# An unrolled two-layer gated FFN on one core: a longer warm-up, six pieces of work moved along the step list, half 1's normalisation shared with ScalarE, and the last half stored tile by tile

## What is computed

```python
x = x + xattn(layernorm(x), token_ids, ctx, ctx, ctx)   # 4 experts, chosen by token id
x = x + ffn(layernorm(x), Wg, W1, W2, W3)               # 8 experts, top 2 by score

def xattn(h, ids, Wg, Wu, Wd):          # Wg = Wu = Wd = ctx, F = D = 256
    e_of = minimum(ids // 3125, 3)
    y_e = (silu(h @ Wg[e].T) * (h @ Wu[e].T)) @ Wd[e].T
    return y_e where e_of == e

def ffn(h, Wg, W1, W2, W3):             # hidden size 176 for each expert
    w = softmax over the two largest of (h @ Wg.T), 0 elsewhere
    return sum over e of w[e] * ((silu(h @ W1[e].T) * (h @ W2[e].T)) @ W3[e].T)
```

## Time and profile before

| what | value |
|---|---|
| median of 3 runs | 166.15 us (165.05 to 166.26) |
| the profiled execution | 166.07 us |
| its span, first to last instruction | 164.3 us |
| PE busy | 153.7 us (94%) |
| DVE busy | 113.8 us (69%) |
| ACT busy | 66.9 us (41%) |
| POOL busy | 58.8 us (36%) |

### The profile page before, as it was taken

One profiled execution on the slowest core, in us unless ns is written; L12 is line 12 of the kernel. 1 busy time (PEld: TensorE's weight loads), 2 busy tenths in 40 slices (PEclk: granted clock), 3 DMA queues, 4 the chain that ended last, 5 costly groups with the idle time before them and its releaser, 6 DMA issues.

```text
span 164.3 us, 2431 instructions
## 1 busy us (share of the span) xinstructions
PE 153.7 (94%) x892; PEld 130.9 (80%) x892; DVE 113.8 (69%) x223; ACT 66.9 (41%) x119; POOL 58.8 (36%) x49
## 2 busy tenths in 40 slices
PE   7399999789998999899999999999999999999991
PEld 2188799768987788688888778898888888888890
DVE  0858999885895867799999796926444744444452
ACT  3366862753518544444438522315222222222210
POOL 0579967369765772459437300000000000000000
PEclk9969999999999999999999999999999999999999
DMA  3976263031130003330000000000000300000003
GB/s 113 345 256 169 70 209 108 0 96 33 70 96 0 2 0 100 96 94 1 0 0 4 0 0 2 0 4 0 0 0 0 129 3 0 0 0 4 2 0 128
DMA packets 4332, 8.76 MB, mean 53 GB/s; under 512 B 736, under 2 KB 864, under 8 KB 4320
## 3 DMA queue, kind: packets, MB, share of 16 engines
q1 hardware_dynamic: 4176, 8.60, 16.6%
q10 hardware_dynamic: 144, 0.00, 0.0%
HBM read 7.55 MB, written 1.05 MB: 52 GB/s over the span
## 4 chain that ended last, share of the span: by engine, by line
PE 63%; DVE 24%; ACT 3%; issue 3%; DMA 3%; POOL 1%; SPq 1%; ACTq 0%; DVEq 0%; POOLq 0%
PE z L675 35%; PE y L700 24%; DVE act_lo L543 5%; DVE act L578 4%; DVE norm L476 3%; DMA raw<-weights_dram 3%; DVE w_lo L549 2%; DVE hT_lo L483 2%; DVE stats L459 2%; PE y L618 1%; DVE x_sb L489 1%; DVE gate_rows L532 1%; ACT act_hi L382 1%; PE y L631 1%; POOL rstd L294 1%
## 5 line engine op out<-in xcount | busy, mean ns | idle before, releaser
L675 PE MATMUL z<-hT_hi,w_hi 128*128 128x512 f32 x120 | 47.7, 397 | 1.0 <-ACT hT_hi L356 0.8
L675 PE MATMUL z<-hT_hi,w_lo 128*128 128x512 f32 x120 | 47.2, 393 | 0.0
L700 PE MATMUL y<-w_hi,act_lo 128*128 128x256 f32 x152 | 43.5, 286 | 1.2 <-DVE act_lo L543 1.2
L543 DVE TENSOR_TENSOR act_lo<-act,act_hi 128x512 fp32r<-128x512 f32 x38 | 32.9, 867 | 14.9 <-ACT act_hi L382 14.7
L700 PE MATMUL y<-w_hi,act_hi 128*128 128x256 f32 x152 | 43.0, 283 | 0.0
L700 PE MATMUL y<-w_lo,act_hi 128*128 128x256 f32 x152 | 43.0, 283 | 0.0
L410 ACT ACTIVATE silu<-z 128x512 f32<-128x512 f32 x38 | 22.6, 596 | 41.7 <-PE z L675 41.6
L675 PE MATMUL z<-hT_lo,w_hi 128*128 128x512 f32 x120 | 37.5, 393 | 0.4 <-DVE hT_lo L483 0.3
L284 POOL TENSOR_TENSOR w_lo<-raw,w_hi 128x768 fp32r<-128x768 f32 (+1 forms) x15 | 28.3, 1891 | 15.0 <-ACT w_hi L347 14.9
L382 ACT CAST act_hi<-act 128x512 fp32r<-128x512 f32 x38 | 23.4, 617 | 23.0 <-DVE act L578 22.7
L700 PEld LDWEIGHTS y<-w_hi,act_lo 128*128 128x128 f32 x152 | 29.0, 191 | 3.3 <-DVE act_lo L543 1.9
(11 more groups left out here) (51 smaller groups left out, 82.0 us busy)
## 6 DMA issues: line engine op xcount, KB each, us to landing
raw<-weights_dram SPq DMA_DIRECT2D x11, 384.0 KB, 3.1
raw<-weights_dram SPq DMA_DIRECT2D x8, 256.0 KB, 4.7
x_sb<-x_dram SPq DMA_DIRECT2D x4, 256.0 KB, 4.7
out_dram<-x_sb SPq DMA_DIRECT2D x4, 256.0 KB, 2.5
consts_sb<-consts_dram SPq DMA_DIRECT2D x1, 68.0 KB, 3.8
ids_sb<-token_ids_dram ACTq DMA_DIRECT2D x1, 4.0 KB, 3.9
router_raw<-router_dram SPq DMA_DIRECT2D x1, 8.0 KB, 2.7
```

Of the source, the lines that this page charges most:

```text
L543: nc.vector.tensor_tensor(act_lo[:, i, :], act[:, i, :], act_hi[:, i, :].bitcast(F32), ALU.subtract)\
L675: return nc.tensor.matmul(bank[:], w[b][:, c, cols], tokens[:, h, k, :], **flags)
L700: last = nc.tensor.matmul(o, a[:, q % BUFFERS, rows], w[b][:, c, wd], start=(first and j == 0), stop=(c == CHUNKS[b] - 1 and j == 2), skip ...
```

## The change

Seven edits. The first six are in the amount of warm-up and in the order and placing of work, the last in how the end is written:

1. WARM goes from 12 to 24 matmuls.
2. GpSimd waits for VectorE's `w_lo` of piece (0, 0) before its own first ones.
3. The normalisation of half 1 in layer 1 (step 4) is shared as in layer 2: two tiles stay on VectorE, two go to ScalarE. With it come one `minus_mean` on VectorE and one `shift` on GpSimd.
4. ROUTER_STEP goes from 6 to 10.
5. The pieces (1, 4) to (1, 10) are split one step later: steps 16 to 22 where it was 15 to 21.
6. `tokens_lo` of layer 2, half 1 goes from step 21 to step 22 on VectorE.
7. The last half is added in four tiles of 256 columns, with one semaphore count for each tile of the last down step, and each tile is stored with a transfer of its own (128 KB), tiles 0 and 2 from SP, tiles 1 and 3 from ScalarE's queue.

```diff
-WARM = 12
+WARM = 24
...
-    "tokens_lo": (6, 4, 5),
+    "tokens_lo": (6, 4, 6),
...
-SPLIT_AT |= {FIRST[1, 0] + c - 5: ((1, c),) for c in range(4, CHUNKS[1])}
+SPLIT_AT |= {FIRST[1, 0] + c - 4: ((1, c),) for c in range(4, CHUNKS[1])}
...
-ROUTER_STEP = 6
+ROUTER_STEP = 10
...
+            for i in (0, 2):
+                t = HALF_TILES + i
+                sp.wait_ge(tile_ready, i + 1)
+                sp.dma_start(out_v[:, t, :], out_sb[:, t, :]).then_inc(stored, 16)
...
             inverse_deviation(0, 0)
+
+            pool.wait_ge(w_lo_vector, 1)
             for c in range(FIRST_PIECES):
...
                 for bb, hh in due("inverse_deviation", q):
                     inverse_deviation(bb, hh)
-                    if bb == 1:
-                        scaled_mean(hh)
+                    scaled_mean(bb, hh)
...
                 for bb, hh in due("normalise", q):
-                    if bb == 1:
-                        normalise_rest(hh)
+                    normalise_rest(bb, hh, (x_sb, x2_sb)[bb])
             round_act(NSTEPS - 1)
+            for i in (1, 3):
+                t = HALF_TILES + i
+                act_e.wait_ge(tile_ready, i + 1)
+                act_e.dma_start(out_v[:, t, :], out_sb[:, t, :]).then_inc(stored, 16)
...
-                        if b == 1:
+                        if ln_no(b, h):
                             nc.vector.tensor_scalar(minus_mean[:, cols], mv[:, cols, 0], -1.0, None, ALU.mult)
...
-                for i, t in list(enumerate(tiles_of(h)))[:DVE_TILES if b else HALF_TILES]:
+                for i, t in list(enumerate(tiles_of(h)))[:DVE_TILES if ln_no(b, h) else HALF_TILES]:
...
-            for i in range(2):
-                if i == 0:
-                    dve.wait_ge(last_first_bank, 1)
-                else:
-                    dve.wait_ge(down_done, NSTEPS)
-                add_bank(1, i, x2_sb, out_sb, out_ready)
+            for i in range(HALF_TILES):
+                t = HALF_TILES + i
+
+                dve.wait_ge(last_tiles, 2 * (i // 2) + 2)
+                nc.vector.tensor_tensor(out_sb[:, t, :], y[1][i // 2][:, (i % 2) * D:(i % 2 + 1) * D], x2_sb[:, t, :],
+                                        ALU.add).then_inc(tile_ready, 1)
...
-                    if q == NSTEPS - 1 and i == 1:
-                        last.then_inc(last_first_bank, 1)
-                last.then_inc(down_done, 1)
+                    if q == NSTEPS - 1:
+                        last.then_inc(last_tiles, 1)
+                if q < NSTEPS - 1:
+                    last.then_inc(down_done, 1)
```

More of the change, by code:

```diff
@@ L199, in ffn_moe @@
         act_hi_done, act_lo_done = sem("act_hi_done"), sem("act_lo_done")
-        down_done, last_first_bank = sem("down_done"), sem("last_first_bank")
+        down_done, last_tiles, tile_ready = sem("down_done"), sem("last_tiles"), sem("tile_ready")
         warm_in, x2_done, out_ready, stored = sem("warm_in"), sem("x2_done"), sem("out_ready"), sem("stored")
@@ L270, in _ @@
                 load_piece(1, c)
-            for pair in range(TILES // 2):
+            for pair in range(TILES // 4):
                 sp.wait_ge(out_ready, pair + 1)
@@ L275, in _ @@
                 sp.dma_start(out_v[:, tiles, :], out_sb[:, tiles, :]).then_inc(stored, 16)
-            sp.wait_ge(stored, 16 * (TILES // 2))
+            for i in (0, 2):
+                t = HALF_TILES + i
+                sp.wait_ge(tile_ready, i + 1)
+                sp.dma_start(out_v[:, t, :], out_sb[:, t, :]).then_inc(stored, 16)
+            sp.wait_ge(stored, 16 * (TILES // 4 + HALF_TILES))
         @block.gpsimd
@@ L295, in inverse_deviation, with scaled_mean @@
                             .then_inc(rstd_done, 1)
-            def scaled_mean(h):
-                pool.wait_ge(rstd_done, ln_part_no(ln_no(1, h), h * HALF_TILES))
+            def scaled_mean(b, h):
+                pool.wait_ge(rstd_done, ln_part_no(ln_no(b, h), h * HALF_TILES))
                 cols = slice(h * HALF_TILES + DVE_TILES, (h + 1) * HALF_TILES)
@@ L356, in tokens_hi, with normalise_rest @@
                     nc.scalar.copy(hT_hi[:, h, k, :], y[h][k][:]).then_inc(hT_hi_done, 1)
-            def normalise_rest(h):
-                act_e.wait_ge(shift_done, h + 1)
-                act_e.wait_ge(rstd_done, ln_part_no(ln_no(1, h), h * HALF_TILES))
-                act_e.wait_ge(norm_T, KD * ln_no(1, h))
+            def normalise_rest(b, h, src):
+                act_e.wait_ge(shift_done, ln_no(b, h))
+                act_e.wait_ge(rstd_done, ln_part_no(ln_no(b, h), h * HALF_TILES))
+                act_e.wait_ge(norm_T, KD * ln_no(b, h))
                 for i in range(DVE_TILES, HALF_TILES):
                     t = h * HALF_TILES + i
-                    nc.scalar.activation(norm[:, i, :], x2_sb[:, t, :], ACT.Identity, bias=shift[:, t:t + 1],
+                    nc.scalar.activation(norm[:, i, :], src[:, t, :], ACT.Identity, bias=shift[:, t:t + 1],
                                          scale=rstd[:, t:t + 1]).then_inc(norm_act, 1)
@@ L623, in transpose_tokens @@
                     for i in range(HALF_TILES):
-                        if b == 0:
-                            pe.wait_ge(norm_done, HALF_TILES * h + i + 1)
+                        n = ln_no(b, h)
+                        if n == 0:
+                            pe.wait_ge(norm_done, i + 1)
                         elif i < DVE_TILES:
-                            pe.wait_ge(norm_done, 2 * HALF_TILES + DVE_TILES * h + i + 1)
+                            pe.wait_ge(norm_done, HALF_TILES + DVE_TILES * (n - 1) + i + 1)
                         else:
-                            pe.wait_ge(norm_act, (HALF_TILES - DVE_TILES) * h + i - DVE_TILES + 1)
+                            pe.wait_ge(norm_act, (HALF_TILES - DVE_TILES) * (n - 1) + i - DVE_TILES + 1)
                         last = nc.tensor.transpose(y[h][k][:, i * P:(i + 1) * P], norm[:, i, k * P:(k + 1) * P], ident)
```

## The result

The changed kernel takes 164.48 us (median of 8 runs, 164.04 to 165.00). The kernel before took 166.14 in the 8 runs beside it (165.05 to 166.26). The ratio is 0.991, with a 95% interval from 0.9885 to 0.9934: 0.9% less, as forecast (164.6). The profiled execution of the changed kernel took 164.04 and is the lowest of its 8, its span is 162.2. So the profiles differ by 2.07 in their spans, and the medians by 1.66. One step of the working was wrong by more than 1 us all the same; two smaller errors, and the difference between the profiled run and the median, made up for it.

A forecast was written before the change was run, and what follows sets the result against it. TensorE was taken to bound the kernel (63% of the chain of waits, VectorE 24%), its stalls lying in the first hundred us. Six terms sum to -1.47: span 164.3 to 162.8, time 164.6 us, range 163.0 to 166.2.

The forecast's parts named there:

- Start: Edits 1 and 2, up to D1: faster clock for the transposes, less the new shift on GpSimd; -0.5, between -0.8 and +0.1.
- rival B: At the start, the clock stays low between 8 and 11 or extra matmuls are slow: 165.2 us; chance 0.15.
- Half 1 of layer 1: Edits 3 and 4, around U8: hT_lo follows hT_hi at once and U8 starts 0.12 earlier; -1.14, between -1.0 and -2.2.
- Step 10: Edit 4, path to D11: the router's subtraction waits for GpSimd ahead of half 0's statistics; +0.76, between -0.4 and +3.0.
- rival A: VectorE's act_lo wins one or both lock races, at 27.3 and 43.4: 163.5 or 162.4 us; chance 0.30.
- Gates: Edit 5, gates and U18: VectorE's copies no longer meet w_lo, U18 starts at about 68.2; -0.97, down to -0.5.
- Step 22: Edit 6, router's matmuls for half 1: three VectorE operations come ahead of hT_lo; +0.68, between +0.3 and +1.3.
- End: Edit 7, last adds and stores: the first store leaves 0.3 earlier, so the last data lands earlier; -0.3, other end +1.1.
- Rival C: GpSimd's operations fall twice into the path to D11: 3.0 instead of 0.76, time 166.9 us; chance 0.10.

The follow-up runs named there:

- the version with step 12: Changed kernel with the router's split in step 12 instead of 10 and tokens_lo of layer 2, half 1 back in step 21: 163.27 us, ratio 0.9862 to before.
- the version with slot 5: Changed kernel with only tokens_lo of layer 2, half 1 put back from step 22 to step 21: 163.56 us, ratio 0.9868 to before.
- step 13: Changed kernel with the router's split in step 13 instead of 10 and tokens_lo of layer 2, half 1 back in step 21: 163.75 us, ratio 0.989 to before.

## Why the prediction was right, and where it was not

**Start (forecast -0.5, measured -0.45): right, under a condition I had put in rival B.** The clock stayed up, `hT_hi` started at 9.31 (I had 8.95), and the wait at D1 grew only from 0.54 to 0.59, since U0 gained 0.69 and not 1.0. The 24 matmuls ended at 8.40, not 8.15, because in this run ten of them ran at the lower clock and in the profile of before nine; the added twelve were all fast. The transposes then started at 8.24 (I had 8.13), and eight of them stand ahead of `hT_hi`, 1.07 where I had left 0.8. The price of `shift` was right (0.26, I had 0.25). That edit 2 costs nothing was wrong: it costs GpSimd 0.2. In this profile VectorE's first `w_lo` came 0.24 earlier than in that of before with 24 matmuls (8.39 and 8.63), which hid this in the sum. What else I got wrong is how often there is something to gain. Most runs of the kernel before that I had seen were of the dropped kind (two of three times near 166.2, the profile too), yet of the 61 later runs in the table 32 were not, and against those edit 1 gains nothing. The Trainium skill, TensorE: Matmul & The Clock Gate, Part 1, had warned that the moment at which the clock changes varies from run to run of one kernel. The runs bear it out: the warm loads change their pace at 4.5 in the profile of before, at 4.99 in that of the changed kernel and at 7.07 in that of the version with step 12.

**Half 1 of layer 1 (forecast -1.14, measured -1.08): right.** `hT_lo` follows `hT_hi`, U8 takes 1.56, and `act_lo` of step 4 lost the port to `gated`, so edit 3 moved nearly nothing. The run with edit 3 undone and the one with the router back confirm which edit did what. Within the term two errors cancel: U8 to D5 shrank by 0.84, not 1.02, and D1 to U8 by 0.24, not 0.12 (0.12 by edit 4, as before with that edit alone shows, and 0.12 by edit 3).

**Step 10 (forecast +0.76, measured -0.40): this is the step that failed.** I wrote that "the cast delays `w_lo` by 0.11, not 0.16, so I keep the order of before". I compared the small delay with the small margin of the earlier trace rows and took VectorE's `act_lo` as fixed. But its time hung on two adds ahead of it, and these waited for TensorE, which edit 4 itself brings 0.5 forward against `act` there. With that wait gone, `act_lo` leads by 0.45, and the stretch comes out at the -0.4 that I had named as the other outcome. The reversed order and the wait that went give 0.92 (18.63 to the 17.71 of the version without the subtraction in that stretch, in which TensorE has next to no wait left); I had put it at 1.2 in the text. The subtraction did meet GpSimd, but its `w_lo` and not the `gated` that I had named, at 0.52 on the path instead of 0.76. So one half of rival A came true, and for a reason: it was no toss-up of 0.16, and of its two races the one at 27.3 went as I had said.

**Gates (forecast -0.97, measured -0.70): right in kind, too large by 0.27.** The copies took 0.63 and TensorE came to them without a wait. But "`gated` is made beside D14" was not so: ScalarE's copy starts when the transposes end (65.02), `gated` ends at 66.39, and D14 is through 0.3 earlier. I had counted D14 at 1.43, as if U18 could follow at once.

**Step 22 (forecast +0.68, measured +0.69): right.** The starts of three VectorE operations, one behind the other, and nothing hidden behind it; the version with slot 5 gives 0.7 back.

**End (forecast -0.3, measured -0.1): too large.** The first store does leave 0.27 earlier, but the transfers are then no faster than the engines, and 1 KB packets keep these busy longer. From the first data packet to the end of the last it is 1.66 (159.31 to 160.97), before 1.56 (161.54 to 163.10):

```profile
160.00:160.50 0.50, 0.00 (x0) 0.00 (x0) 0.00 (x0) 0.00 (x0) 0.00 (x0) 1.00 1.04 336
```

The DMA engines are busy all the time (1.04 by the window) at 336 GB/s, against 0.96 at 361 in the earlier trace rows. The other end of my range, +1.1 (each half-sized packet as long as a whole one), did not come either.

**The sum.** The terms measured add up to -2.05, mine to -1.47. Step 10 alone is -1.16 of the difference, the gates and the end give back 0.27 and 0.2. The medians moved by 1.66, less than the profiles, because the changed kernel's profiled run was its best, 0.44 under the median, and that of before only 0.07 under. So the forecast of 164.6 is near 164.48 largely by luck: an error of 1.16 at step 10, 0.46 the other way at the gates and the end, and 0.4 that the profiles and the medians differ by. The shape of the rivals served better than the sum: rival A, with one race won, had the mechanism.

Rival B (clock) fell as a story of this profile, but half of it holds for the comparison: before often starts with the clock up. Rival C fell: GpSimd was in the way once, not twice.

## What to carry to other kernels

Where two engines race for a shared port, don't look at the margin between the two starts alone. Follow each back to the last event they have in common, here `act` of step 9, and ask which waits on the way the change removes. A helper that needs a whole slot of another engine (a subtraction of 16 columns cost TensorE 0.95 in steps 4 to 8 at the one place, 0.5 at another, 0.2 in step 12) is best moved to where the engine that reads it has slack on both sides, and one number moved rightly was worth more here than six other edits.

## What the runs showed of the hardware that I had not expected

**The warm matmuls don't last the same from run to run.** The same 24 took 6.93, 7.03 to 7.29, 7.83, 8.07 and 8.21 us in the profiled runs, all at a granted clock that the profile gives as 1.00. The longest, of the version with the router in step 12:

```profile
1.17 8.21 PE L720 MATMUL z<-warm_sb 128*128 128x512 bf16 x24 [1.17 <-DVE warm_sb L561]
...
6.27 0.15 PEld L720 LDWEIGHTS z<-warm_sb 128*128 128x128 bf16 x1 [0.28 <-issue]
6.70 0.15 PEld L720 LDWEIGHTS z<-warm_sb 128*128 128x128 bf16 x1 [0.28 <-issue]
7.07 1.83 PEld L720 LDWEIGHTS z<-warm_sb 128*128 128x128 bf16 x9 [0.22 <-issue]
...
9.22 0.60 PE L627 MATMUL y<-consts_sb,gate_rows 128*128 128x128 f32 x4
```

and of the changed kernel's first profile:

```profile
4.56 0.15 PEld L720 LDWEIGHTS z<-warm_sb 128*128 128x128 bf16 x1 [0.28 <-issue]
4.99 2.92 PEld L720 LDWEIGHTS z<-warm_sb 128*128 128x128 bf16 x14 [0.28 <-issue]
```

(PEld are the weight loads; `...` stands for rows left out.) Each matmul has its weight load, so the loads give the pace: one in 0.43 up to 6.70 in the one run and up to 4.99 in the other, then one in 0.21 (2.92 for 14). 0.43 for 512 columns is the 1.2 GHz level, though the column has the granted clock at 1.00 from the start. The records from which the column is made begin only at 7.00 in the one trace and at 5.01 in the other, where the pace changes. So the column is not to be trusted before the clock has first changed; the spacing is. When the clock rises late, the 24 run past the point at which the gates' transposes are ready (8.03 in the earlier trace rows) and these start at up to 9.22; U0 is then up to 1.0 later and D1 up to 0.7. That is some 0.7 of the spread of 1.04 of the changed kernel (163.96 to 165.00). I have it from profiles of different kernels with the same start, so it is a likely cause of the spread, not a shown one; a run with some 16 to 20 warm matmuls was not tried.

**Half-sized packets took a little over half the time.** A tile of 256 columns is stored in rows of 1 KB, the pair in rows of 2 KB. From the windows: 0.5 us x 16 engines x 1.04 over 336 GB/s x 0.5 us / 1 KB is about 51 ns for one; with 0.96 and 361 of the earlier trace rows about 87 ns for one of 2 KB. The packets of the last stores themselves average 48.6 ns (512 of 1 KB) and 86.5 ns (256 of 2 KB). So 1 KB packets were slower per byte by 12 to 17%, and this lengthens the last data by 0.1 of the 0.27 that the earlier first store wins.

**A loss of the port costs what is left of the other engine's operation.** The subtraction of 16 columns took 1.54, 1.23 and 0.66 at three places, by what GpSimd was in the middle of: in the changed kernel it ends at 44.32 and GpSimd's `w_lo` at 44.29, with step 13 at 54.76 and GpSimd's `gated` at 54.72; `act_lo` took 0.68, 1.37, 1.50, 1.78 or 2.24.
